# Splitting the experts' bias rows on VectorE in the first stage, making the gate columns three steps earlier, and putting the last weight fold behind the last products

## The reference, cut to what matters

```python
h = patches(x) @ W.T + b                          # 12544 tokens, 768 -> 256
h = h + scan(layernorm(h))                        # Bu -> x = A_bar*x + Bu -> y = x W_C + u W_D + biases
n = layernorm(h)
y1 = ln(n + mha(n), g1, be1)                      # 196 sequences of 64 tokens, 4 heads
gates = softmax(y1 @ wg); idx = argmax(gates)     # 8 experts, capacity S // 8
hid = disp @ w1 + b1;  y = hid @ w2 + b2          # no nonlinearity between w1 and w2
h = h + ln(y1 + gate * y[slot], g2, be2)
```

## Time and profile before

| | |
|---|---|
| median of 3 runs | 1286.43 us (1283.87 to 1287.28) |
| the profiled execution, its own time | 1285.87 us |
| its span in the profile | 1284.0 us |
| PE busy in the span | 1183.7 us (92%) |
| DVE busy | 1010.5 us (79%) |
| POOL busy | 857.0 us (67%) |
| ACT busy | 720.8 us (56%) |
| first stage, first to last product | 28.9 to 546 us |
| second stage, from its first load | 547.9 us |

### The profile page before, as it was taken

How to read it: one execution, slowest core, us unless ns; L and a number is a source line. 1 busy time by engine, 2 the same in 40 slices (tenths; PEclk the granted TensorE clock), 3 DMA queues, 4 the chain that set the end, 5 groups by cost and what they waited for, 6 DMA issues and landing times. The chain is left out here.

```text
span 1284.0 us, 37111 instructions
## 1 busy us (share of the span) xinstructions
PE 1183.7 (92%) x11134; PEld 1086.1 (85%) x11135; DVE 1010.5 (79%) x2957; ACT 720.8 (56%) x1518; POOL 857.0 (67%) x1159
## 2 busy tenths in 40 slices
PE   1999999999999999749999999999999984999994
PEld 1999999999999999749999999999999973666662
DVE  4688888888888888705778877877788776699997
ACT  3455566566565655415555555555555540678885
POOL 1566666666666666373777777777777773378887
PEclk9999999999999999978999999999999996999997
DMA  7435555545454542211333333333233325788882
GB/s 221 165 126 157 173 155 177 164 146 172 141 184 149 179 148 90 91 42 39 113 104 110 107 107 102 110 105 110 98 111 107 110 92 157 207 236 241 238 235 93
DMA packets 97304, 180.11 MB, mean 140 GB/s; under 512 B 12319, under 2 KB 62753, under 8 KB 96226
## 3 DMA queue, kind: packets, MB, share of 16 engines
q1 hardware_dynamic: 82500, 138.66, 36.0%
q0 software_dynamic: 13312, 39.75, 8.3%
q10 hardware_dynamic: 1440, 1.07, 0.3%
HBM read 112.69 MB, written 67.80 MB: 141 GB/s over the span
## 5 line engine op out<-in xcount | busy, mean ns | idle before, releaser
L528 POOL TENSOR_TENSOR xl<-xf,xh 128x512 fp32r<-128x512 f32 x141 | 183.8, 1332 | 178.0 <-ACT xh L447 178.0
L311 PE MATMUL ps_h<-wh,xh 128*128 128x256 f32 x588 | 166.3, 283 | 4.9 <-DVE xl L669 4.9
L311 PE MATMUL ps_h<-wh,xl 128*128 128x256 f32 x588 | 166.1, 282 | 0.0
L311 PE MATMUL ps_h<-wl,xh 128*128 128x256 f32 x588 | 165.3, 281 | 0.0
L1061 POOL DMA_INDIRECT bins<-rows,slot_i x98 | 109.8, 1120 | 72.8 <-DVE rows L1172 54.0
L1462 POOL DMA_INDIRECT out<-res,c_idx x106 | 123.8, 1168 | 43.3 <-issue 21.4
L947 ACT ACTIVATE q<-b,cols_c 128x256 f32<-128x256 f32 x98 | 41.1, 471 | 158.8 <-PE ps_v L1291 155.1
L311 PE MATMUL b<-x2h,wh 128*128 128x256 f32 x392 | 120.6, 308 | 2.8 <-DVE x2l L1078 2.8
L1610 PE MATMUL c_ps_y<-w,yt 128*128 x424 | 117.9, 401 | 3.3 <-ACT yt L1409 1.7
L311 PEld LDWEIGHTS ps_h<-wh,xh 128*128 128x128 f32 x588 | 111.4, 189 | 5.7 <-DVE xl L669 5.7
L311 PEld LDWEIGHTS ps_h<-wh,xl 128*128 128x128 f32 x588 | 111.4, 190 | 0.0
(11 more groups left out here) (282 smaller groups left out, 4258.0 us busy)
## 6 DMA issues: line engine op xcount, KB each, us to landing
xf<-xt SPq DMA_DIRECT2D x49, 768.0 KB, 5.4
row<-bins SPq DMA_DIRECT2D x106, 257.5 KB
h_dram<-h1b SPq DMA_DIRECT2D x49, 256.0 KB, 5.4
x_dram<-x2o SPq DMA_DIRECT2D x49, 256.0 KB, 5.6
x<-x_dram SPq DMA_DIRECT2D x98, 128.0 KB, 2.8
rows<-h_dram SPq DMA_DIRECT2D x98, 128.0 KB
w1s<-w1t SPq DMA_DIRECT2D x8, 1024.0 KB, 6.8
w2s<-w SPq DMA_DIRECT2D x8, 516.0 KB, 5.9
```

The lines of the kernel that those rows point to most:

```text
L311: last = nc.tensor.matmul(out_ps, a, b, start=(i == 0), stop=(i == len(terms) - 1))
L528: last = nc.gpsimd.tensor_tensor(xl[:, p, part], xf[:, p, part], xh[:, p, part].bitcast(F32), ALU.subtract)
```

## The change

Four things are changed.

1. **Split of the bias rows.** The five POOL instructions at the start of the second stage go. Instead DVE splits each expert's row as soon as it is made, four dependent instructions of 2 x 256 behind L665, in slot 1.
2. **Gate columns.** `gate_weights` moves on DVE from the end of step 51 to the end of step 49, its scratch from `w1s` to the patch buffers `xf`, which are free by then. PE's part is cut in two: `gate_first` at the end of its step 50, `gate_second` at the end of 51, ahead of the last `outputs`. The copies on ACT and DVE move likewise.
3. **Last fold.** Expert 7 is no longer folded in steps 42 to 45 but behind everything else that PE does in the stage; ACT copies it as its last instruction.
4. PE's loop ends at step 42 instead of 48; the rest is written out.

```diff
-                flat = w1s[:, free[0] - size:free[0]]
+                flat = xf[:].rearrange("p s c -> p (s c)")[:, free[0] - size:free[0]]
...
ACT:
-                    if k.slot(FOLD) == 4 and k.valid(FOLD * NE):
+                    if k.slot(FOLD) == 4 and k.valid(FOLD * (NE - 1)):
...
-                    if isinstance(k.t, int) and k.c == NG + 3:
+                    if isinstance(k.t, int) and k.c == NG + 2:
                         act.wait_ge(turned, 1)
...
                 run(act, step, 0, NG + 5, 6, 42, FOLD)
-                act.wait_ge(wog_out, 1)
-                nc.scalar.activation(gate_part(wh, W_OUT + D, OS), wog[:], ACT.Copy).then_inc(g_hi, 1)
+                act.wait_ge(fold_ps, NE)
+                nc.scalar.activation(w12[:, NE - 1, :], ps_f[:], ACT.Copy).then_inc(fold_out, 1)
DVE, fold_bias:
                         v.tensor_tensor(row, ps_fb[:], row, ALU.add).then_inc(fb_out, 1)
+                        wait(dve, fb_out, e + 1)
+                        v.tensor_copy(two, row).then_inc(fb_split, 1)
+                        wait(dve, fb_split, e * 4 + 1)
+                        v.tensor_tensor(row, row, two.bitcast(F32), ALU.subtract).then_inc(fb_split, 1)
+                        wait(dve, fb_split, e * 4 + 2)
+                        v.tensor_scalar(row, row, half[:, 1:2], None, ALU.mult).then_inc(fb_split, 1)
+                        wait(dve, fb_split, e * 4 + 3)
+                        v.scalar_tensor_tensor(two, two.bitcast(F32), half[:, 0:1], row, ALU.mult,
+                                               ALU.add).then_inc(fb_split, 1)
DVE, step:
+                    if isinstance(k.t, int) and k.c == NG:
+                        gate_weights()
                     if isinstance(k.t, int) and k.c == NG + 2:
-                        gate_weights()
+                        gate_low()
PE, step:
-                    if k.valid(FOLD * NE):
+                    if k.valid(FOLD * (NE - 1)):
                         fold(k)
...
+                    if isinstance(k.t, int) and k.c == NG + 1:
+                        gate_first()
+                    if isinstance(k.t, int) and k.c == NG + 2:
+                        gate_second()
+                run(pe, step, 0, NG + 4, 6, 42, FOLD)
+                for c in range(FOLD):
+                    fold(At(0, FOLD * (NE - 1) + c, FOLD))
POOL, second stage:
-                g.tensor_copy(b12s[:], b12[:]).then_inc(split_b, 1)
-                pool.wait_ge(split_b, 1)
-                g.tensor_tensor(b12[:], b12[:], b12s[:].bitcast(F32), ALU.subtract).then_inc(split_b, 1)
-                pool.wait_ge(split_b, 2)
-                g.tensor_scalar(b12[:], b12[:], half[:, 1:2], None, ALU.mult).then_inc(split_b, 1)
-                g.tensor_scalar(b12s[:], b12s[:].bitcast(F32), half[:, 0:1], None, ALU.mult).then_inc(split_b, 1)
-                pool.wait_ge(split_b, 4)
-                g.tensor_tensor(b12s[:], b12s[:].bitcast(F32), b12[:], ALU.add)
```

More of the change, by code:

```diff
@@ L365, in build @@
             h1b_done = a_sem("a_h1b_done")
-            w2_first, acc_done = (a_sem(n) for n in ("w2_first_loaded", "fold_bias_sum"))
+            w2_first, acc_done, fb_split = (a_sem(n) for n in ("w2_first_loaded", "fold_bias_sum", "fold_bias_split"))
             HALF = FK // 2 * D
@@ L511, in step @@
                         nc.scalar.activation(gate_part(wh, W_QKV + 3 * D, QS), gg[:], ACT.Copy).then_inc(g_hi, 1)
+                    if isinstance(k.t, int) and k.c == NG + 3:
+                        act.wait_ge(wog_out, 1)
+                        nc.scalar.activation(gate_part(wh, W_OUT + D, OS), wog[:], ACT.Copy).then_inc(g_hi, 1)
                 run(act, step, 0, NG + 5, 6, 42, FOLD)
-                act.wait_ge(wog_out, 1)
-                nc.scalar.activation(gate_part(wh, W_OUT + D, OS), wog[:], ACT.Copy).then_inc(g_hi, 1)
+                act.wait_ge(fold_ps, NE)
+                nc.scalar.activation(w12[:, NE - 1, :], ps_f[:], ACT.Copy).then_inc(fold_out, 1)
             @blk.gpsimd
@@ L785, in fold_sum, with gate_first, gate_second @@
                         nc.tensor.matmul(ps_fb[:], ones_2[:], acc[:], start=True, stop=True).then_inc(fb_ps, 1)
+                mm, ps_g = nc.tensor.matmul, ps_h[0]
+                def gate_first():
+                    pe.wait_ge(fold_out, NE - 1)
+                    pe.wait_ge(h_done, 2 * NG)
+                    pe.wait_ge(pre_in, 2)
+                    for t in range(FT):
+                        for i in range(FT):
+                            last = nc.tensor.transpose(ps_f[:, t * D + i * P:t * D + (i + 1) * P], wo[:, i, t * P:(t + 1) * P], ident[:])
+                    last.then_inc(turned, 1)
+                    pe.wait_ge(pre_in, 5)
+                    for t in range(FT):
+                        mm(ps_g[:, FT * NE:(FT + 1) * NE], ones_f[:], gg[:, t, :], start=(t == 0), stop=(t == FT - 1))
+                    for t in range(FT):
+                        mm(ps_g[:, (FT + 1) * NE:(FT + 2) * NE], spread[:, t, :], wg_sb[:, t, :], start=(t == 0), stop=(t == FT - 1))
+                    for t in range(FT):
+                        mm(ps_g[:, (FT + 2) * NE:(FT + 3) * NE], spread[:, FT + t, :], gg[:, t, :], start=(t == 0), stop=(t == FT - 1))
+                def gate_second():
+                    pe.wait_ge(turned_out, 1)
+                    for i in range(FT):
+                        for t in range(FT):
+                            last = mm(ps_g[:, i * NE:(i + 1) * NE], wo_t[:, t, i * P:(i + 1) * P], gg[:, t, :],
+                                      start=(t == 0), stop=(t == FT - 1))
+                    last.then_inc(wog_ps, 1)
                 def step(k):
@@ L876, in build @@
             row_ranks = sem("b_row_ranks")
-            split_b = sem("b_split_bias")
             h1_tok, x2_tok = (a.rearrange("(l j s t) d -> t j l s d", l=L, j=NG, s=2, t=2) for a in (h1_dram, x2_dram))
```

40 lines of the change are left out of this document (10 added, 30 removed).

## The result

The changed kernel takes 1301.3 us in the median of 4 runs (1299.58 to 1301.71); the kernel before, on the same chip, 1285.6 (1283.87 to 1287.28). The ratio is 1.0119, with a 95% interval of 1.0104 to 1.0134: slower by 15.7 us, forecast +8.3. The sign is right; the median lies 6.6 above the forecast and just above the range's upper end of 1301. The profiled execution took 1301.58 us with a span of 1299.8, 15.8 more than the span before.

A forecast was written before the change was run, and what follows sets the result against it. PE was taken to bound most of the first stage, DVE close behind, POOL the second stage's start; 12.0 - 1.0 + 9.0 - 11.7 = +8.3 gave 1294.7 us, 8-in-10 range 1278 to 1301.

The forecast's parts named there:

- Part 1a: First stage, experts 0 to 5: the split on DVE costs 2.0 us each, +12.0 (0 to +20).
- The three meetings: Slot 2: L641 and both DVE scans fall into POOL's three `xl`, 3.3 us at most for each expert.
- my upper bound by the Trainium skill: First stage: a meeting could cost a full `xl`, 1.3 us instead of 1.1; 3.6 more in all, 1298.
- DVE absorbs the split: Rival for the first stage: a split under 1.2 us costs 0; -6.7 in all, 1280 us; chance 0.30.
- One meeting only: Rival for the first stage: one scan of each expert falls behind one `xl`, 5 us; about 1286; chance 0.12.
- everything collides and the clock stays low: Rival: 20 for the cycles, no gain in steps 42 to 47, 13 at the end; +21, 1308 us; chance 0.08.
- Part 3: Steps 42 to 47: the last fold leaves, but DVE is now the bound; -1 us (-7 to 0).
- Parts 2 and 3: End of the first stage: gate's new order and last fold at full length on the path; +9.0 us (+4 to +14).
- rival of the hidden fold: Stage end: if stores landed later than ACT's copy, it costs 3 less, 1291 us; inside the forecast's 0.50.
- Part 1b: Start of the second stage: without POOL's split, PE's 8.16 us idle and 3.5 of half clock go; -11.7 (-8 to -12.5).
- Part 4: End of PE's first-stage loop: ending it earlier, with steps written out, costs nothing.

The follow-up runs named there:

- e7: Kernel before, with the split's five large POOL instructions laid into POOL's idle stretches of the second stage's first three steps; 1276.0 us, ratio 0.9922.
- e1: Changed kernel with the split of the bias rows back on POOL, in one piece at the second stage's start; 1290.3 us, ratio 1.0042 to the kernel before.
- e6: Kernel before with the gate's part of the change alone; last fold stays in steps 42 to 45, split on POOL; 1296.8 us, ratio 1.0077.
- e2: Kernel before with only the split moved to DVE, right behind the add of the bias row; 1291.7 us, ratio 1.0067.
- e4: Kernel before with the split still on POOL, but one expert's rows behind each of POOL's first eight second-stage steps; 1288.0 us, ratio 1.0028.
- e9: Kernel before with the split in POOL's second-stage gaps, last fold in halves around the gate's last products, gate scratch in `xf`; 1272.0 us, ratio 0.9904.
- e10: Changed kernel with POOL's `xl` in six instructions of 256 columns a group instead of three of 512; 1281.9 us, ratio 0.9981 to the kernel before.

## Why the prediction came out as it did

**Part 1a, the split on DVE: right in mechanism, 2.4 too small against the profile of before.** Price of one: 2.08 us from the start of L670 to that of L659 (355.58 to 357.66), less the add's 0.35 of before, 1.7; I took 1.5. The three meetings are there: 0.9 on L645 and 2.1 on the scans. A fourth, 1.1 on L614 beside POOL's `hb`, I had not named; it stands right ahead of the `ul` that PE waits for. Against the kernel before it is 2.6 a cycle, not 2.0, and 14.4 up to step 42, not 12.0; PE waits for `ul` in slot 2 (0.91), and DVE stretches slots 2 and 5. Part of the 2.6 is the threshold in slot 5: against e7's cycle the split costs 1.9, and 11.4 up to step 42, close to my 12.0. That slot 5 stood at such a threshold already I had not seen, though it is of the same kind as the one I priced.

By the Trainium skill ("SBUF — State Buffer", Who interferes with whom) a DVE instruction with two SBUF inputs, or a copy, cast or `tensor_scalar` in a two-port mode, and a GpSimd instruction that reads SBUF exclude each other for a whole instruction. The runs agree with it: L645 on 128x2 loses 0.9 us, a copy of 2x256 1.0, while L641 (one SBUF input, 0.15) and `ul` (PSUM and SBUF, 0.68) lose nothing; and halving POOL's instructions took most of the loss away. The full `xl` of 1.3 us for each meeting, my upper bound by the Trainium skill, was not paid: the rows give 0.9 to 1.1, as I had read from the one meeting of before.

**The rivals.** "DVE absorbs the split" is wrong; its condition was a split under 1.2 us. "One meeting only" is wrong too. Of "everything collides and the clock stays low" one sign came, L645 (its L641) waits in every slot 2 from 60 to 500 us, and the other did not, as the fold ran at full clock; its 13 for the end was nearer than my 9.0, its 20 for the cycles was not.

**Part 3, last fold out of steps 42 to 45: right.** -1.75 against -1, since DVE bounds those steps. e1 shows the gain when it does not: -5.8.

**Parts 2 and 3, the end: this is the step that failed, +14.7 against +9.0 (and its range of +4 to +14).** By its terms: `inputs`(48) came 5.1 later against step 48, forecast 3.9; 0.8 of the difference is the last split's copy, which met POOL's `h1b` (1.12 instead of 0.28). From there to the last `outputs` I had 12.3 and it was 15.9 (547.74 to 563.61), and this is the larger part of the miss. I had allowed for 1.5 of half clock there at the most, but the half clock held from `inputs`(48), ahead of which PE had stood 6.65 us, through `gate_first` and the whole of `outputs`(47). The wait for ACT's copy, which stands behind these, was sized too low as well, 3.29 against 2.3. On the last `outputs` the half clock came as I had it: 4.3 us (563.61 to 567.88) for 2.9, and I had put 1.5. From the last `outputs` to ACT's last copy it was 12.0, forecast 9.6 and this 1.5; the 0.9 that is left is the fold, 7.1 at full clock. I had priced it at 6.1, although my own 1.74 for a slot in part 3 gives 7.0. The next stage's first transposes came 4.5 behind that copy, about as far as behind the end that I had taken before (547.25 to 551.87).

And one reason was wrong although its number did no harm. I charged the last fold at its full length, since "all engines meet there". It did end last, so the chain is right, but beside it runs the last group's statistics and store, so that leaving it out would save only 1.5 us (e6 against e1). The gate's early place, which I had seen as three small items, is 9.4 by itself. The rest of the 14.7, 5.3, is the last row's split: the changed kernel against e1. Alone, in e2, it lengthened the end by 1.3; together with the gate's preparation PE stands 6.65 us ahead of `inputs`(48) instead of 4.16, and is at half clock from there to 559, where in e1 it was from 530 to 534 and from 541 to 547. What each of these two is worth was not separated. The rival of the hidden fold described this; I had it inside the forecast, with no weight of its own.

**Part 1b, POOL rid of the split: right.** -10.9 by the fifth group and -12.4 with the rest that was not followed up, forecast -11.7. There is no wait ahead of the third group's transposes; from the second group's to them it is 7.9 us, before it was 16.3.

**Part 4, the loop's end:** nothing in the profile speaks against 0; no run has it alone.

**Sum.** +2.4 from the cycles, -0.75 from steps 42 to 48, +5.7 from the end, -0.7 from the second stage, +0.9 ahead of step 2: 7.5 over the forecast in the span, 6.6 in the medians. Of what I said would show it: a scan over 1.5 us (two in 3.48), a cycle near 63.5 (64.0), six steps near 60 (60.0), the first load 28.1 us later than 547.85 where I had 18 to 22. The last is the one that missed. The last fold did not end before the last store had landed, as far as the rows show it: with no fold behind, the first load goes out 2.7 us after the last store's issue (here 571.87), and here it went out at 575.92, 0.3 behind the end of the fold's copy. L637 of slot 3 (now L641, 370.13) stands 2.9 us behind `turn_u` (367.25), where before it stood 0.1 ahead, 3.0 later as forecast.

## What to carry to other kernels

Where two engines shut each other out for a whole instruction, look for the window in which the other one is idle, and count what no longer fits into it; the bill is set by the length of the other engine's instruction, so cutting that one can be worth more than moving or shortening one's own (here one loop bound, 18 us). Work that is taken off the head of a stage may go back into that engine's own waits a step or two later, before it goes to a busy engine; but in the steady part there may be no room for it (e4). At the end of a pipeline, ask for each piece whether it stands ahead of the last products or behind them: ahead it is paid in full, and in these traces a wait of 3.3 to 6.7 us added half clock to what followed; behind them it runs beside the last group's statistics and store and costs what overhangs (1.5 us in e1, 3.5 in e9).

## What the runs showed of the hardware that I had not expected

- The loss in a meeting with a POOL instruction of about 1.3 us does not depend on the size of the instruction that waits: 128x2 lost 0.9 us (L645, 1.07 instead of 0.16), 2x256 lost 1.0 (CAST, 1.31 instead of 0.28), a scan of 128x256 about 1.0 (two in 3.48 instead of 1.39).
- On POOL `xl` of a group takes 3.8 us in three instructions and 4.2 in six where nothing meets it, and 4.2 and 4.7 in the median group of the changed kernel and of e10.
- The same first stage (before, e4, e7) runs its cycle in 61.4 or in 62.1 us, by one meeting in slot 5; over six cycles that is 4 us, about the spread of the runs of before on one chip (1282.4 to 1288.3); that the one makes the other is not shown.
- POOL on two partitions: 1.88 us for a copy of 2x2048, 4.5 for a subtraction, 5.45 for a scaling; one expert's five instructions on 2x256 take 3.9, so eight of them take 31 against 22 in one piece.
